# A fused attention and expert layer: four loop orders, and a set-up that fetches the first four head pairs in two parts

## The reference, cut to what matters

```python
h = layernorm(x) * (1 + ca) + sa                 # sa, ca, ga, sb, cb, gb: silu(c) @ wmod
q, k, v = split(h @ W_attn + b_attn)             # q and k scaled by 16 ** -0.5
phi = lambda u: exp(u @ omega - 0.5 * sum(u * u)) / sqrt(m)
S, Z = cumsum(phi(k) v^T), cumsum(phi(k))        # causal linear attention
y = (phi(q) . S) / (phi(q) . Z + EPS)
x = x + ga * (y @ W_proj + b_proj)
h = layernorm(x) * (1 + cb) + sb
w = top2(softmax(h @ Wg^T + bg))                 # weights of the two experts used
out_e = relu(h @ Wi^T + (h @ A_e^T) @ B_e^T) @ Wo^T
x = x + gb * sum_e w_e * out_e
```

## Time and profile before

| what | value |
|---|---|
| three runs | 791.97, 792.42, 794.87 us |
| the profiled execution | 791.14 us, span 788.9 us |
| mean granted clock of TensorE | 0.991 |
| busy: PE / DVE / ACT / POOL | 740.5 / 526.3 / 422.1 / 62.7 us |

### The profile page before, as it was taken

One profiled execution on the slowest core, in us unless ns is written; L12 is line 12 of the kernel. 1 busy time (PEld: TensorE's weight loads), 2 busy tenths in 40 slices (PEclk: granted clock), 3 DMA queues, 4 the chain that ended last, 5 costly groups with the idle time before them and its releaser, 6 DMA issues.

```text
span 788.9 us, 17005 instructions
## 1 busy us (share of the span) xinstructions
PE 740.5 (94%) x6138; PEld 605.5 (77%) x6138; DVE 526.3 (67%) x1265; ACT 422.1 (53%) x769; POOL 62.7 (8%) x72
## 2 busy tenths in 40 slices
PE   3889999999999999999999999999999999999696
PEld 3678768887698867887688876987678876987466
DVE  4366776676666776766776767767766767766456
ACT  3376636664556554665366745575456644564232
POOL 1260010001000010001000010000100010000100
PEclk9999999999999999999999999999999999999799
DMA  8750183103801065102811057010741029000000
GB/s 282 198 143 2 54 211 64 53 0 118 205 2 53 27 188 111 53 0 80 208 38 53 0 146 179 9 44 27 212 87 53 0 89 223 13 29 28 0 1 27
DMA packets 42804, 65.36 MB, mean 83 GB/s; under 512 B 5000, under 2 KB 19104, under 8 KB 42656
## 3 DMA queue, kind: packets, MB, share of 16 engines
q1 hardware_dynamic: 42784, 65.09, 30.6%
HBM read 39.91 MB, written 25.17 MB: 82 GB/s over the span
## 4 chain that ended last, share of the span: by engine, by line
PE 79%; DVE 12%; issue 3%; DMA 2%; ACT 2%; POOL 1%; DVEq 0%; SPq 0%; ACTq 0%; POOLq 0%
PE pa L579 11%; PE prod L592 7%; PE ring L428 6%; PE ring L558 5%; PE pa L428 5%; PE pa L430 5%; PE pa L429 5%; PE ring L430 4%; PE ring L429 4%; PE ring L612 4%; PE ring L563 3%; PE ring L720 2%; PE ring L619 2%; PE pa L693 2%; DVE am_phk L1178 2%
## 5 line engine op out<-in xcount | busy, mean ns | idle before, releaser
L579 PE MATMUL pa<-phq,phkT 128*128 128x128 f32 x768 | 101.2, 275 | 0.0
L1178 DVE TENSOR_TENSOR am_phk<-pa,const 128x512 f32<-128x512 f32 x112 | 77.0, 688 | 35.6 <-PE pa L579 34.6
L579 PEld LDWEIGHTS pa<-phq,phkT 128*128 128x128 f32 x768 | 95.4, 192 | 2.1
L1348 DVE SCALAR_TENSOR_TENSOR am_phk<-ring,am_phk 128x512 f32<-128x512 f32 x64 | 44.3, 691 | 53.2 <-PE ring L773 53.2
L988 ACT ACTIVATE qk_r<-phq 128x512 fp32r<-128x512 f32 x64 | 40.5, 633 | 63.7 <-DVE phq L1357 63.7
L428 PE MATMUL pa<-wo_r,qk_r 128*128 128x256 f32 x256 | 72.2, 282 | 0.6 <-DVE qk_l L1353 0.6
L430 PE MATMUL pa<-wo_l,qk_r 128*128 128x256 f32 x256 | 72.3, 282 | 0.0
L429 PE MATMUL pa<-wo_r,qk_l 128*128 128x256 f32 x256 | 72.0, 281 | 0.0
L558 PE MATMUL ring<-xq,omega_x 100*128 100x512 f32 x196 | 70.3, 440 | 1.4 <-DVE lora_w L1171 1.4
L918 ACT ACTIVATE phq<-ring 128x512 f32<-128x512 f32 x82 | 49.3, 602 | 36.1 <-PE ring L558 34.9
L918 ACT ACTIVATE phkT<-ring 128x512 f32<-128x512 f32 x98 | 58.3, 595 | 12.9 <-PE ring L558 12.6
(11 more groups left out here) (209 smaller groups left out, 1609.3 us busy)
## 6 DMA issues: line engine op xcount, KB each, us to landing
xq<-qk_parts SPq DMA_DIRECT2D x48, 512.0 KB
qk_parts<-qk_r SPq DMA_DIRECT2D x32, 256.0 KB, 4.4
qk_parts<-qk_l SPq DMA_DIRECT2D x32, 256.0 KB, 4.9
tok<-in_L_attn_x SPq DMA_DIRECT2D x8, 512.0 KB, 3.6
xr<-in_L_attn_x SPq DMA_DIRECT2D x8, 512.0 KB, 3.4
out_x<-tg SPq DMA_DIRECT2D x16, 256.0 KB, 2.2
norm_parts<-norm_r SPq DMA_DIRECT2D x16, 128.0 KB, 2.3
norm_parts<-norm_l SPq DMA_DIRECT2D x16, 128.0 KB, 2.4
```

Of the source, the lines that this page charges most:

```text
L579: mm = pe.matmul(score_bank(q, a)[:, tt], phkT[:, q % 2, a, tt], query(q)[:, a, tt], start=True, stop=True)
L1178: dve.tensor_tensor(am[:, 2 * (q % 2) + a, :].rearrange("p (c t) -> p c t", c=NT), score_bank(q, a)[:].rearrange("p (c t) -> p c t", c=NT) ...
L1348: dve.scalar_tensor_tensor(r2[:, f % 2, :], z_bank[f % 4][:], 0.0, rho, ALU.max, ALU.mult).then_inc(r2_done.sem, 1)
```

## The change

Four orders in the loop:

1. `masks(n)` moves from behind `base(n, 3)` to between its two halves.
2. In the experts' turns PE issues base(f + 2) behind z2(f - 1) and the feature tiles, no longer ahead of them. `AHEAD` has no tiles in turn 2 and two in turn 3; from turn 4 on each turn has one, as far as turn 8, then two and one, as before from turn 5 on. ACT takes the exponentials of a turn's tiles one turn later (`AHEAD.get(f - 1)`), the last one after all turns.
3. `split_qk(n + 1, 1)` moves ahead of the last `divide` on DVE.
4. `finish` works on the first half of the tokens as soon as the last wo of that half is done (`wo_first`), and adds each half's residual before it goes on.

The set-up: the modulation weights are loaded ahead of x, x comes in two halves; the silu is done first on ACT and DVE; omega is loaded ahead of `wi`; gates are computed one at a time between the q/k products, in the banks `pb`; `wi` is turned before the lead; the values come inside the lead; the lead has three banks. What SP fetches for the lead is only pairs 0 and 1 (`lead_moved`), half of what `moved[0]` stood for; pairs 2 and 3 follow, and PE waits for them at its first tile beyond the lead. The DRAM buffers have another layout, so that `norm_parts` is written by four small transfers for each half (before: two of 64 rows each) and read by one (before: two). The loop uses this layout too.

```diff
-AHEAD = {0: 1, 1: 1, 2: 2, 3: 1, 5: 1, 6: 1, 7: 1, 8: 1, 9: 2, 10: 1}
+AHEAD = {0: 1, 1: 1, 3: 2, 4: 1, 5: 1, 6: 1, 7: 1, 8: 1, 9: 2, 10: 1}
...
-            load(ld_x, (tok[:], x_rows[0]))
-            load(ld_const, (const[:], consts))
             w_rows = lambda w, k, cols: w[k * P:(k + 1) * P, cols]
             load(ld_mod[0], *((wmod_raw[0][k], w_rows(wmod, k, slice(0, 2 * C))) for k in range(KT)))
+            for b in range(2):
+                load(ld_x[b], (tok[:, 2 * b:2 * b + 2, :], x_rows[0, :, 2 * b:2 * b + 2, :]))
+            load(ld_const, (const[:], consts))
...
+            def send_norms(n, half):
+                for part, src in enumerate((norm_r, norm_l)):
+                    for kind in range(2):
+                        row = (2 * half + kind) * VA
+                        sp.dma_start(norms_out[half, part, :, :, kind].rearrange("a g i t -> (a g) i t"),
+                                     src[row:row + 2 * GROUP, :].bitcast(F32)).then_inc(norm_out[half].sem, 16)
...
+            def first_front():
+                send(0, 0)
+                send(0, 1)
+                wait(sp, norm_split, 0, 1)
+                send_norms(0, 0)
+                fetch_qk(0, 0, first, lead_moved)
+                fetch_norms(0, 0, first, lead_moved)
+                send(0, 2)
+                send(0, 3)
...
                 wait(pe, low_high, n, 1)
-                base(n, 3)
+                base(n, 3, [0])
+                masks(n)
+                base(n, 3, [1])
...
-                    if 4 <= f + 2 < FT:
-                        base(n, f + 2)
                     if 1 <= f <= FT:
...
                         for _ in range(AHEAD.get(f, 0)):
                             features(n + 1, tile // TILES, [tile % TILES])
                             tile += 1
+                    if 4 <= f + 2 < FT:
+                        base(n, f + 2)
                     if f >= 3:
...
-            pe.wait_ge(wa_low.sem, KT)
-            pe.wait_ge(set_mod.sem, 2)
...
+            pe.wait_ge(ld_mod[1].sem, 16 * KT)
+            setup_gate(0)
             norms(0, 0)
             qk(0, 3)
...
+            for q in range(4):
+                setup_wi(q)
+            features(0, 0, range(RUN), lead=True)
+            values(0)
+            features(0, 0, range(RUN, TILES), lead=True)
+            pe.wait_ge(ld_wo.sem, 16 * KT)
+            pe.wait_ge(late_vec.sem, 4)
+            setup_wo(0)
+            setup_wo(1)
+            features(0, 1, range(RUN), lead=True)
+            setup_low()
+            setup_lora(0)
+            features(0, 1, range(RUN, TILES), lead=True)
+            setup_lora(1)
+            pe.wait_ge(late_act.sem, 5)
+            setup_wo(2)
+            pe.wait_ge(late_vec.sem, 7)
+            setup_wo(3)
...
-                    for _ in range(AHEAD.get(f, 0) if front_next else 0):
+                    for _ in range(AHEAD.get(f - 1, 0) if front_next else 0):
                         features(n + 1, tile // TILES, [tile % TILES])
                         tile += 1
...
+            def setup_wo(q):
+                dve.wait_ge(late_pe.sem, (5, 6, 10, 11)[q])
+                two = slice(2 * q, 2 * q + 2)
+                high = wo_r[:, two, :].rearrange("p t c -> p (t c)")
+                dve.tensor_copy(high, wo_bank[q][:]).then_inc(wo_high.sem, 1)
+                dve.wait_ge(wo_high.sem, q + 1)
+                dve.tensor_tensor(wo_l[:, two, :].rearrange("p t c -> p (t c)"), wo_bank[q][:],
+                                  high.bitcast(F32), ALU.subtract).then_inc(late_vec.sem, 1)
...
+                if front_next:
+                    split_qk(n + 1, 1)
                 divide(n, GROUPS - 1)
-                if front_next:
-                    split_qk(n + 1, 1)
```

More of the change, by code:

```diff
@@ L330, in _ @@
             sp.sem_inc(scaled.sem, scaled.per)
[L332 to L356, removed]
@@ L358, in next_front @@
-            def next_front(n):
[L360 to L390, removed]
-                wait(sp, norm_split, n, 2)
[L392 to L396, removed]
@@ new lines, in _ @@
+            first, second, both = slice(0, 1), slice(1, 2), slice(0, 2)
+            def first_front():
[7 more added lines that the diff above has]
+                send(0, 3)
+                wait(sp, norm_split, 0, 2)
+                send_norms(0, 1)
+                fetch_qk(0, 0, second, moved[0])
+                fetch_norms(0, 0, second, moved[0])
+                fetch_qk(0, 1, both, moved[1])
+                fetch_norms(0, 1, both, moved[1])
@@ L445, in setup_mods, with setup_gate @@
                 mm.then_inc(mods_ps.sem, 1)
[L447 to L456, removed]
+            def setup_gate(q):
+                for b in range(B):
+                    for k in range(KT):
+                        mm = pe.matmul(pb[q][:, b * C:(b + 1) * C], s_rep[:, k, b, :],
+                                       wmod_raw[1][k][:, (3 * q) * C:(3 * q + 1) * C],
+                                       start=k == 0, stop=k == KT - 1)
+                mm.then_inc(gates_ps.sem, 1)
             def transpose1(n, after=None):
@@ L545, in features @@
                     tile = p * TILES + k
-                    dst = lead_bank[tile % 4] if lead else proj_bank(tile)
-                    if tile == 0:
+                    dst = lead_bank[tile % 3] if lead else proj_bank(tile)
+                    if tile == 0 and lead:
+                        pe.wait_ge(lead_moved.sem, 4 * 16)
+                    if tile == 0 and not lead:
                         wait(pe, moved[0], n, moved[0].per)
@@ L550, in features @@
                         wait(pe, moved[1], n, moved[1].per)
-                    if lead and tile >= 4:
-                        wait(pe, exp_done, n, tile - 3)
+                    if tile == 0 and lead:
+                        pe.wait_ge(late_vec.sem, 2)
+                    if lead and tile >= 3:
+                        wait(pe, exp_done, n, tile - 2)
                     if not lead and 2 <= tile < 2 * TILES:
@@ L906, in features @@
                     tile = q * TILES + k
-                    bank_of = lead_bank[tile % 4] if lead else proj_bank(tile)
+                    bank_of = lead_bank[tile % 3] if lead else proj_bank(tile)
                     wait(act, proj_ps, n, tile + 1)
@@ L988, in ffn @@
                         act.activation(g_r[:, k % 3, :], g[:, k % 4, :], ACT.Copy).then_inc(g_high.sem, 1)
-            normalize_rest(0)
+                while front_next and tile < 2 * TILES:
+                    features(n + 1, tile // TILES, [tile % TILES])
+                    tile += 1
             setup()
```

267 lines of the change are left out of this document (142 added, 125 removed).

## The result

The changed kernel takes 1081.03 us (median of 4 runs, 1080.53 to 1083.35) against 792.19 us of the kernel before beside it: a ratio of 1.364, 95% interval 1.361 to 1.367. The forecast was 799.

The account below looks back on a forecast made before the run. The prediction took PE to bound the kernel, with 79% of the chain. From 791.1 us it added 13.4 for seven loop blocks, took off 2.1 for the last block and 3.8 for the set-up: 798.6, given as 799.0, range 788 to 807.

Parts of the forecast that it names:

- The step that rests on it: Loop, norms' writes on SP: first starts near 294.5, last lands at 299.3 to 299.6; a saving of 0.5 us.
- The prediction's own sign of being wrong: A period at or below the present one, or PE idle ahead of z1(0) until a transfer ends; no size given.
- Rival (c): Ahead of z1(0): dear small transfers keep `mask_low` waiting until 301.3, 1.5 us a block, 809 us; chance 0.09.
- the dear bound: Norms' writes: 0.64 us of SP each, the last landing at 301.3, delaying DVE by 1.6 us and PE by 1.0.
- Rival (d): PE's clock falls in the turns' stalls, 1.6 us each, once a block 11 us: 810 us; chance 0.03.
- Turns: Turns 4 and 9: PE waits for ACT's later exponentials, costing 1.27 and 1.55 us a block; first turns gain 0.2.
- Masks, projection, finish: PE's waits ahead of z1(0) and the projection go, 0.5 and 0.2 us a block; tail 1.4 us shorter, once.
- Set-up: Before the loop: lead at 35.5, first tiles beyond it at 50.5 instead of 54.25; 3.8 us less, bounds 0.3 and 6.
- Sum: Whole kernel: 791.1 + 13.4 - 2.1 - 3.8 = 798.6 us, given as 799.0 for the measured median.

## Why the prediction was wrong

Wrong by 282 us through one step that has no number in it at all. The prediction lists what is removed, moved and added, and for the transfers it has only "The loop now writes the norms in eight transfers, not four." That the q/k writes go to a new layout too, in a new shape, is in the diff and in SP's order, and I priced it at nothing, without a word on what hides it. It costs 275 us alone (1067.8 less 792.8, the kernel before with the layout), and 283 in the change (1081.0 less 798.2). The step that rests on it failed with it: norms that land at 298.7 to 301.3 need an SP that is free from 294.5 on and writes that land after 2.2 to 2.4 us. In the third block of the changed kernel SP stood behind q/k writes for some 30 us, from 260.1 to 289.95, and the last norms landed at 304.05. The prediction's own sign of being wrong, an idle moment ahead of z1(0) that ends with a transfer, is what the profile shows.

Rival (c) had the place right, `mask_low` waiting for the norms, and the wrong price: 1.0 us where it was 33. Its reason, small transfers at the dear bound, is not what made the 33. It was true only of the wait left when the q/k writes were cut: 0.30 us for 8 x 512, below my 0.35 to 0.4, and 0.58 to 0.63 for the 4 x 2 x 512 that the change uses, which is near the dear bound of 0.64. I had asked what their size costs and not what their shape does. Rival (d), the clock, came true behind the waits of 33 us, and in some blocks behind two waits of about 1.1 us within 3; not behind the turns' stalls, for which I had weighed it: the run with the whole change and wide transfers has all 14 of them and a mean clock of 0.991, as before.

What was priced held, but for the size of the set-up's gain:

- *Turns*: stalls at tiles 4 and 10, waiting for ACT, 0.94 and 1.34 for 1.17 and 1.45. The two pairs of runs that differ in the turns alone give 15.5 us (802.2 - 786.7) and 17.8 (798.2 - 780.5); my net was 7 x 2.62 = 18.3.
- *Masks, projection, finish*: 6.8 us for 7.0.
- *Set-up*: lead at 33.7 instead of 35.5, tiles beyond it at 48.9 instead of 50.5, with wide transfers; 6.2 us gained for 3.8. I had halved the old fetch of 10.14 us, and PE waited 1.34 for the new one. In the changed kernel they came at 52.01 and 77.07.
- *Sum*: 798.2 for 799.0, once the transfers are wide.

The Trainium skill, page "DMA: Bandwidth & Descriptors", section "Why a DMA increments its semaphore by 16 and not by 1", says that the number of engines is the largest up to 16 that divides the slowest dimension longer than one on both sides. The windows agree, with 0.13 for 2 and 0.26 for 4. The prediction cites another section of this page, "Anatomy of one DMA", for a time per byte. That section gives it for transfers issued from GpSimd, and SP issues these; it has no term for shape, and I asked it about the set-up's fetches and about no write of the loop.

## What to carry to other kernels

A new layout of a buffer is a new shape of every transfer to and from it: list them by their outermost dimension before and after, and price each, even where the bytes stay the same. Where a strided piece makes the outermost dimension small, cut the transfer so that many rows are outermost in each; twice the transfers took 259 us off here. And a slow transfer was not cured here by moving it behind others: find who reads its result, and who writes over its source.

## What the hardware showed that I had not expected

- The rate of the q/k writes follows the outermost dimension and nothing else that was varied: 51 GB/s at 2, 102 at 4, so 25.5 for each engine's worth of busy share; at 64 it is 203, at a share of 0.87.
- SP is held at issue when narrow writes are under way: the first two of four take 0.5 to 1.1 us, the later two 3.3 to 7.9, and the norms' writes behind them 5.6 for two. Nothing here shows what they wait for.
- The issue of a small write costs SP by its pattern, 0.30 us for 8 x 512 and 0.58 for 4 x 2 x 512. Yet 64 x 512 takes 0.60 and 128 x 512, twice as much, mostly 0.32 to 0.44 in the same kernel. Why is open.
- A wait of 33 us leaves PE at a granted clock of 0.50, which is 1.2 GHz, for the next 9 us: a 512-column product takes 0.63 at 308.73 and 0.39 again at 314.93. Single waits of 0.94, 1.34 and once 2.29 us leave no trace in it; two of about 1.1 us close together sometimes do.
